# A layer norm's variance moved to tokens on partitions, and the last stage's weight preparation moved into the attention before it

## The reference

```
mu  = mean(x, axis=-1);  var = mean(square(x - mu))
xn  = (x - mu) * rsqrt(var + LN_EPS) * gamma + beta
q, k, v = xn @ Wq + bq, xn @ Wk + bk, xn @ Wv + bv      # 8 heads
x = x + softmax(q k^T / sqrt(dk)) v                     # summed over groups, reshaped
```

```
z = sigmoid(x_t @ W_z + h @ U_z + vz);  r = sigmoid(x_t @ W_r + h @ U_r + vr)
h = (1 - z) * h + z * tanh(x_t @ W + (r * h) @ U + vh)
gate = h @ Wg + routing_bias                            # top 4 of 8 experts, swiglu
```

## Time and profile before

| | us |
|---|---|
| median of 3 runs | 2818.0 (2813.54 to 2818.51) |
| the profiled execution | 2814.62 |
| its span, first to last instruction | 2812.6 |
| layer norm block | from 1415.8 to 1468.4 |
| attention block | to 1636.3 |
| weights block | to 1657.1 |
| rows block | to 1668.4 |

### The profile page before, as it was taken

The page is one execution under the profiler, slowest core; times in us unless marked ns, Lnnn a source line. Parts: engine busy times, 40 slices in busy tenths (PEclk is TensorE's granted clock), DMA queues, the critical chain, the costliest instruction groups (busy, mean ns, idle before and its releaser), DMA issues. The chain is left out here.

```text
span 2812.6 us, 119114 instructions
## 1 busy us (share of the span) xinstructions
PE 2424.7 (86%) x50764; PEld 2022.1 (72%) x50764; DVE 1965.6 (70%) x7376; ACT 1144.6 (41%) x3659; POOL 431.1 (15%) x404
## 2 busy tenths in 40 slices
PE   1678999999999999987547846999999999999999
PEld 0455677777777777654216636999999999999998
DVE  4567777777777777787578736777766777777775
ACT  3124555555555555566126623333333333333333
POOL 0000000000000000000029910222222222222222
PEclk9778999999999999999669967999999999999999
DMA  5000000000000000000013332000000000000000
GB/s 166 2 2 2 5 5 5 5 5 5 5 5 5 5 5 5 5 5 4 3 69 87 88 90 57 9 9 9 11 9 9 9 9 9 9 9 9 5 5 6
DMA packets 52745, 53.77 MB, mean 19 GB/s; under 512 B 24678, under 2 KB 46839, under 8 KB 50041
## 3 DMA queue, kind: packets, MB, share of 16 engines
q1 hardware_dynamic: 47284, 27.79, 3.6%
q0 software_dynamic: 2000, 14.68, 1.5%
q10 hardware_dynamic: 2934, 3.69, 0.4%
HBM read 39.59 MB, written 6.55 MB: 16 GB/s over the span
## 5 line engine op out<-in xcount | busy, mean ns | idle before, releaser
L103 PE MATMUL p<-g_hl,m_h 128*128 128x128 f16 x3072 | 528.7, 219 | 0.0
L103 PE MATMUL p<-g_hh,m_h 128*128 128x128 f16 x3072 | 528.7, 219 | 0.0
L103 PE MATMUL p<-g_hh,m_l 128*128 128x128 f16 x3072 | 528.6, 219 | 0.0
L765 DVE STREAM_TRANSPOSE gt<-lg_b 128x512 f32<-128x512 f32 x324 | 230.3, 711 | 216.5 <-PE lg_b L448 202.6
L1928 POOL TENSOR_TENSOR a_l<-a,a_h 128x384 f16<-128x384 f32 x256 | 233.9, 914 | 915.9 <-ACT a_h L1886 915.9
L642 ACT ACTIVATE gl<-gt 128x128 f32<-128x128 f32 x324 | 100.2, 309 | 629.2 <-DVE gt L765 629.1
L657 ACT ACTIVATE hm<-xy,b 128x512 f32<-128x512 f32 x512 | 347.4, 678 | 0.1
L103 PEld LDWEIGHTS p<-g_hh,m_h 128*128 128x128 f16 x3072 | 300.4, 98 | 1.8
L103 PEld LDWEIGHTS p<-g_hh,m_l 128*128 128x128 f16 x3072 | 300.6, 98 | 0.7
L103 PEld LDWEIGHTS p<-g_hl,m_h 128*128 128x128 f16 x3072 | 300.7, 98 | 0.0
L448 PE MATMUL lg_b<-a_wh_hi,lh 128*32 128x256 f16 x4096 | 217.4, 291 | 79.0 <-DVE lh L789 76.8
(11 more groups left out here) (421 smaller groups left out, 6900.7 us busy)
## 6 DMA issues: line engine op xcount, KB each, us to landing
m_stage<-in_m_w POOLq DMA_DIRECT2D x12, 1024.0 KB, 5.3
hs<-in_m_w SPq DMA_DIRECT2D x16, 384.0 KB, 3.2
xs<-in_x POOLq DMA_DIRECT2D x1, 2048.0 KB, 8.4
x_dram<-x SPq DMA_DIRECT2D x16, 128.0 KB, 2.2
s_v<-in_l_wv SPq DMA_DIRECT2D x1, 2048.0 KB
attention_dram<-att SPq DMA_DIRECT2D x16, 128.0 KB, 2.7
attr<-attention_dram SPq DMA_DIRECT2D x128, 16.0 KB, 1.7
x2r<-x_dram SPq DMA_DIRECT2D x16, 128.0 KB, 2.5
```

The costliest lines, as they stand in the source:

```text
L103: ins = pe.matmul(out, w[wp](k), x[xp](k), start=start, stop=last and k == KT - 1 and xp == 1, skip_group_check=True)
L765: dve.transpose(gt[:, :], lg_b[slot // QS % 2][:, :, :, :].rearrange("p g a x -> p (g a x)"))\
```

## The change

**Layer norm.** The mean is made and subtracted as before, for all four tiles first and in place. ScalarE squares. The variance is made with the squares as the stationary matrix and one column of `mean_w` moving, so that each token's variance stands on its own partition: 16 columns for 2048 tokens, 32 products. Root, reciprocal and Newton step work on 128x16. VectorE multiplies the result with the identity matrix, 128 tokens at a time, into diagonal matrices, and PE multiplies these by `mean_w`, which spreads each token's value over all partitions, into the bank that held the mean. The factor 1/256 is taken out by `gscale` = 256 gamma. ScalarE adds beta. The splits of q and k come before the reductions of v.

```diff
+            NB = W // P
+            sq = [prob[:, :, :, :].rearrange("p k s n -> p k (s n)"),
+                  st.enter_context(nc.sbuf_tensor("ln_sq", [P, KT, W], F32))[:, :, :]]
+            diag = [sq[j // 2][:, j % 2, :] for j in range(NJ)]
+            va, y, yy = (st.enter_context(nc.sbuf_tensor("ln_" + n, [P, NJ * NB], F32)) for n in ("va", "y", "yy"))
...
+            gscale = st.enter_context(nc.sbuf_tensor("ln_gscale", [P, KT], F32))
+            mean = [b[:, :, :].rearrange("p s n -> p (s n)") for b in sc]
+            var = pj[:, :, :].rearrange("p s n -> p (s n)")
...
                 for j in range(NJ):
-                    if j + 1 < NJ:
-                        means(j + 1)
                     pe.wait_ge(sq_ready, j + 1)
-                    if j >= 2:
-                        pe.wait_ge(va_ready, j - 1)
-                    for k in range(KT):
-                        last = pe.matmul(var[j % 2], mean_w[:, :], sq[:, k, :], start=(k == 0), stop=(k == KT - 1))
+                    for u in range(NB):
+                        n = j * NB + u
+                        for k in range(KT):
+                            last = pe.matmul(var[:, n:n + 1], sq[j % 2][:, k, u * P:(u + 1) * P], mean_w[:, 0:1],
+                                             start=(n == 0 and k == 0), stop=(k == KT - 1), skip_group_check=True)
                     last.then_inc(var_pe, 1)
+                pe.wait_ge(d_ready, NJ)
+                for j in range(NJ):
+                    pe.wait_ge(turned, j + 1)
+                    pe.matmul(mean[j], mean_w[:, :], diag[j], start=True,
+                              stop=True).then_inc(spread, 1)
...
-                    if j >= 1:
-                        act.wait_ge(var_pe, j)
-                    act.activation(sq, dd[:, j % 2], ACT.Square).then_inc(sq_ready, 1)
-                    act.wait_ge(var_pe, j + 1)
                     if j >= 2:
-                        act.wait_ge(scaled, 2 * (j - 1))
-
-                    act.activation(va[:, j % 2, :], var[j % 2], ACT.Relu, bias=eps[:, :]).then_inc(va_ready, 1)
-                    act.wait_ge(va_ready, j + 1)
-                    act.activation(root[:, j % 2, :], va[:, j % 2, :], ACT.Sqrt).then_inc(root_ready, 1)
+                        act.wait_ge(var_pe, j - 1)
+                    act.activation(sq[j % 2], x(j), ACT.Square).then_inc(sq_ready, 1)
                 act.wait_ge(loaded, 16 * len(loads))
+                for n, (src, hi, _lo) in enumerate(jobs[:2]):
+                    act.activation(hi, src, ACT.Copy, scale=S).then_inc(hi_done, 1)
+                act.wait_ge(var_pe, NJ)
+
+                act.activation(va[:, :], var[:, 0:NJ * NB], ACT.Relu, bias=eps[:, :]).then_inc(va_ready, 1)
+                act.wait_ge(va_ready, 1)
+                act.activation(y[:, :], va[:, :], ACT.Sqrt).then_inc(root_ready, 1)
                 act.wait_ge(v_sum, KT + 1)
                 act.wait_ge(ready, 3)
-                for src, hi, _lo in jobs:
+                for src, hi, _lo in jobs[2:]:
                     act.activation(hi, src, ACT.Copy, scale=S).then_inc(hi_done, 1)
-
-            @block.gpsimd
-            def _(pool):
-                pool.wait_ge(affine, 32)
+                act.wait_ge(affine, 32)
                 for j in range(NJ):
                     for k in range(KT):
-                        pool.wait_ge(scaled, 2 * j + k + 1)
-                        pool.tensor_scalar(x(j)[:, k, :], xg[:, k, :], beta[:, k:k + 1], None, ALU.add).then_inc(kept, 1)
+                        act.wait_ge(scaled, 2 * j + k + 1)
+                        act.activation(x(j)[:, k, :], x(j)[:, k, :], ACT.Identity, bias=beta[:, k:k + 1])
 
             @block.vector
             def _(dve):
-                def centre(j):
-                    if j >= 2:
-                        dve.wait_ge(sq_ready, j - 1)
-                        dve.wait_ge(scaled, 2 * (j - 1))
-                    dve.wait_ge(mean_pe, j + 1)
-                    dve.tensor_tensor(dd[:, j % 2], x(j), mean[j % 2].unsqueeze(1).to_broadcast([P, KT, W]),
-                                      ALU.subtract).then_inc(d_ready, 1)
+                def low(n):
+                    src, hi, lo = jobs[n]
+                    dve.wait_ge(hi_done, n + 1)
+                    dve.scalar_tensor_tensor(out=lo, in0=src, scalar=S, in1=hi, op0=ALU.mult,
+                                             op1=ALU.subtract).then_inc(lo_done, 1)
 
                 dve.memset(mean_w[:, :], 1.0 / D).then_inc(ready, 1)
 
                 dve.memset(eps[:, :], 4 * LN_EPS).then_inc(ready, 1)
                 dve.memset(brow[:, :], 0.0).then_inc(ready, 1)
                 dve.memset(ones2[:, :], 1.0)
+                for j in range(NJ):
+                    dve.wait_ge(mean_pe, j + 1)
+                    dve.tensor_tensor(x(j), x(j), mean[j].unsqueeze(1).to_broadcast([P, KT, W]),
+                                      ALU.subtract).then_inc(d_ready, 1)
                 dve.wait_ge(affine, 32)
-                centre(0)
-                for j in range(NJ):
-                    if j + 1 < NJ:
-                        centre(j + 1)
-                    v, y = va[:, j % 2, :], root[:, j % 2, :]
-                    dve.wait_ge(root_ready, j + 1)
-                    if j >= 1:
-                        dve.wait_ge(scaled, 2 * j)
-                    dve.reciprocal(y, root[:, j % 2, :]).then_inc(steps, 1)
-
-                    dve.wait_ge(steps, NST * j + 1)
-                    dve.tensor_tensor(yy[:, :], y, y, ALU.mult).then_inc(steps, 1)
-                    dve.wait_ge(steps, NST * j + 2)
-                    dve.scalar_tensor_tensor(out=yy[:, :], in0=yy[:, :], scalar=-0.5, in1=v, op0=ALU.mult,
-                                             op1=ALU.mult).then_inc(steps, 1)
-                    dve.wait_ge(steps, NST * j + 3)
-                    dve.scalar_tensor_tensor(out=y, in0=yy[:, :], scalar=1.5, in1=y, op0=ALU.add,
-                                             op1=ALU.mult).then_inc(steps, 1)
-                    dve.wait_ge(steps, NST * j + 4)
-                    if j >= 1:
-                        dve.wait_ge(kept, 2 * j)
-                    for k in range(KT):
-                        dve.scalar_tensor_tensor(out=xg[:, k, :], in0=dd[:, j % 2, k, :], scalar=gamma[:, k:k + 1],
-                                                 in1=y, op0=ALU.mult, op1=ALU.mult).then_inc(scaled, 1)
+
+                dve.tensor_scalar(gscale[:, :], gamma[:, :], float(D), None, ALU.mult).then_inc(steps, 1)
                 dve.wait_ge(loaded, 16 * len(loads))
-
+                dve.tensor_reduce(s_b[0:1, 2 * D:3 * D], s_b8[0:1, :, :], AX_X, ALU.add).then_inc(v_sum, 1)
+                for n in range(2):
+                    low(n)
                 for k in range(KT):
                     dve.tensor_reduce(s_v[:, k, :], s_v8[:, k, :, :], AX_X, ALU.add).then_inc(v_sum, 1)
-                dve.tensor_reduce(s_b[0:1, 2 * D:3 * D], s_b8[0:1, :, :], AX_X, ALU.add).then_inc(v_sum, 1)
-                for n, (src, hi, lo) in enumerate(jobs):
-                    dve.wait_ge(hi_done, n + 1)
-                    dve.scalar_tensor_tensor(out=lo, in0=src, scalar=S, in1=hi, op0=ALU.mult,
-                                             op1=ALU.subtract).then_inc(lo_done, 1)
+                dve.wait_ge(root_ready, 1)
+                dve.reciprocal(y[:, :], y[:, :]).then_inc(steps, 1)
+
+                dve.wait_ge(steps, 2)
+                dve.tensor_tensor(yy[:, :], y[:, :], y[:, :], ALU.mult).then_inc(steps, 1)
+                dve.wait_ge(steps, 3)
+                dve.scalar_tensor_tensor(out=yy[:, :], in0=yy[:, :], scalar=-0.5, in1=va[:, :], op0=ALU.mult,
+                                         op1=ALU.mult).then_inc(steps, 1)
+                dve.wait_ge(steps, 4)
+                dve.scalar_tensor_tensor(out=y[:, :], in0=yy[:, :], scalar=1.5, in1=y[:, :], op0=ALU.add,
+                                         op1=ALU.mult).then_inc(steps, 1)
+                dve.wait_ge(steps, 5)
+                for j in range(NJ):
+                    dve.tensor_tensor(diag[j].rearrange("p (u n) -> p u n", n=P), ident[:, :].unsqueeze(1).to_broadcast([P, NB, P]),
+                                      y[:, j * NB:(j + 1) * NB].unsqueeze(2).to_broadcast([P, NB, P]),
+                                      ALU.mult).then_inc(turned, 1)
+                for n in (2, 3):
+                    low(n)
+                for j in range(NJ):
+                    dve.wait_ge(spread, j + 1)
+                    for k in range(KT):
+                        dve.scalar_tensor_tensor(out=x(j)[:, k, :], in0=x(j)[:, k, :], scalar=gscale[:, k:k + 1],
+                                                 in1=mean[j], op0=ALU.mult, op1=ALU.mult).then_inc(scaled, 1)
```

(82 more changed lines are left out.)

171 lines of the change are left out of this document (56 added, 115 removed).

## The result

The changed kernel takes 2802.4 us (median of 8 runs, 2792.9 to 2808.4), the kernel before 2815.1 beside it. The medians are 12.7 us apart (0.5%); the ratio on record, which is not the quotient of the medians, is 0.9929 with a 95% interval of 0.9904 to 0.9953 (0.7%, 20 us). It is faster, by a third to a half of the forecast gain of 38 us, and its median lies 12 us above the upper end of the forecast range. The profiled execution took 2808.4 us with a span of 2806.6, 6.0 less than before.

What follows compares the result with a forecast made beforehand. VectorE was taken to set the layer norm's time; weights and rows blocks ran beside nothing. Layer norm -18.6, attention +10.3, weights block -20.8, rows block -1.7, first piece -6.9 sum to -37.7 us: forecast 2777, own range 2772 to 2782.

Steps and rivals of the forecast that it cites:

- The layer norm's size: Layer norm block: reciprocal and Newton step once on 128x16 make it 18.6 us shorter (ends -14 and -21).
- The weights block: Block preparing the last stage's weights, beside which nothing runs: it goes, -20.8 us.
- the first piece: Last stage's first step: ScalarE's 6.95 us wait for the first piece of `m_w3` goes, -6.9 us.
- C: Layer norm: variance at half clock throughout, root at 1443, +5 us, 2782; chance 0.09.
- D: Attention: PE at half clock throughout, +60 us, 2837; chance 0.01.
- E: Last stage's first step finds another stall of 7 us, so the boundary gains don't come, 2784; chance 0.05.
- One of the signs that I had named for a wrong forecast: Attention: the forecast is wrong if the clock there is more than 0.05 lower.
- Attention gets the work that was moved: Attention block: loads, low parts, `vps` and PE's warmer start together add 10.3 us (ends +3 and +22).
- Low parts on VectorE: Attention's batch 2: seven low parts, 3.7 us pitch plus 4.9 waiting, less 1.8 slack: +6.8 us (ends +1 and +13).
- rival A: Attention: low parts wait for the rest of GpSimd's instruction, 11 us for five, with a clock dip +9, 2786; chance 0.19.
- `vps`, +3.6: Attention at g = 58: product takes 4.5 us at full clock, some 0.9 absorbed: +3.6 us (ends +2 and +8).
- PE enters warm: Attention's start: PE comes from the spreading matmuls, perhaps warm, where the first 3 us ran at half clock: -0.5 us.

Runs made afterwards that it cites:

- the three pairs of profiles above: Batches 2 to 7 with low parts beside GpSimd against without: 129.8 and 133.2 us against 116.0, and 130.7 against 117.0.
- the hold run: Changed kernel with GpSimd held before its fifth piece until VectorE has written the seven low parts: 2785.3 us, 0.9886.
- `vps` at the end: Changed kernel with the `vps` product issued behind the last `values` product of attention: 2789.9 us, 0.9898.
- in lots: Changed kernel with the 36 `vps` instructions split into six lots of six, behind the projections of g = 57 to 62: 2794.9 us, 0.9927.
- the first wait: GpSimd's first operation held until VectorE has split x for batches 0 and 1: changed kernel 2796.4 us (0.9910); kernel before with new layer norm 2797.5 us (0.9910).
- the run with the block alone: Kernel before with only the new layer norm block, the last stage's weights staying in their own block: 2809.2 us, 0.9970.
- the four profiles with 17.8: Four of nine profiled kernels, the same program up to g = 16, whose second batch took 17.8 us; in the others 21 to 24.
- memsets: GpSimd's three operations on every weight piece replaced by memsets: changed kernel 2779.0 us (0.9852), kernel before 0.9994, kernel before with new layer norm 2800.3 us (0.9917).

## Why the prediction was wrong

**Right.** The layer norm's size (-19.6 for -18.6): of the 64 variance instructions the first 16 took 1.84 us, the next 3.06 and the last two lots 3.55 each, so the clock fell earlier than I had it, by 16 instructions. The root came at 1439.6; the block began 2.2 us later than before, so this is 1437.4 on the forecast's clock, for 1438. The weights block (-20.8), the rows block (-1.3 for -1.7) and the first piece (-7.1 for -6.9) came as worked out; rivals C, D and E are out, E by the 3.06 us between the first two `zr`. One of the signs that I had named for a wrong forecast came: attention's clock fell by 0.13, to 0.77, not by at most 0.05.

**The step that failed is "Attention gets the work that was moved": 10.3 us in the sum, with an upper end of 22, where 39.7 came.** In its terms:
- *Low parts on VectorE, +6.8 with an upper end of 13.* They cost 14 to 17 us, by the three pairs of profiles above. The forecast took 3.7 us of pitch plus 0.98 us of waiting for each of five. Pitch cost nothing (the hold run), and the waits were 16.1 us over all seven (11.1 with `vps` at the end, 11.1 with it in lots, 9.9 with the first wait), the two small ones too, for which none was put down: `s_rl` alone lost 2.9. I had the right mechanism in rival A and chose the median extra of an `xn_l` over it; the eight `xn_l` hold two of 1.07 that met no wait. The pair of instructions in which I saw the two-input rule agree with the trace was an `xn_h`, which has one input, so it spoke for the other kind of wait. A's 11 us for five lies nearer to the 12.2, 8.0, 8.0 and 9.0 that the five took in the same runs, but by luck in part: it takes a 5.4 us instruction of GpSimd's as closed to its end, and it is not (last section). With some 3.5 us of it closed, A's formula gives an estimate of 1.4 us for a wait, 7 for five and 10 for seven.
- *What follows from it.* PE waits longer and its clock goes from 0.84 to 0.63 in the third batch; I put 3 us on a dip. The third batch is no sum of waits: it took 36.7 us with 16.1 of them and 37.3 with 11.1. How the rest divides between ScalarE's waits, PE's clock and the later splits stays open.
- *`vps`, +3.6, at full clock "that the last batch has".* It had it for 2.6 us. The product took 7.0 us in the changed kernel (1635.46 to 1642.46), ScalarE waited 7.36 us for a transpose, and the batch grew by 9.3. This is just past the bound of 8 that I kept for half clock: the clock of a stretch was carried over to work of another kind put into it, and the clock stayed low behind it (0.60 from 1642.46 on).
- *"PE enters warm", -0.5.* Here a cost lay that no term had: the first batch's 2.9 us, and in this profile some 10 to 13 of the 27.0 in batches 2 to 7, what is left of them without the low parts' 14 to 17. The layer norm block was costed to its end, and its gain taken as kept. The first splits met GpSimd's chain in a new phase; in the run with the block alone that took back 16 of 19.6 us (7 in the first batch, 9 in the next six), and one wait on GpSimd returned it. The forecast had GpSimd's start in it ("at most 7.9 us later"), but asked only whether GpSimd would be late, not whom it would meet.

Put together: 27.0 and 9.3 for 6.8 and 3.6, and 2.9 for the first batch, give 2777 + 20.2 + 5.7 + 3.4 = 2806; the profiled execution took 2808.4, the blocks ahead 2.2 of it. These are whole batches as measured, so it proves no cause that the sum closes. Runs of the changed kernel came in two lots, 2793 to 2798 and 2807 to 2808. The one profile is of the upper lot. Its second batch holds an `xn_h` of 5.78 and an `xn_l` of 3.85 us where the four profiles with 17.8 have at most 1.4 and 1.1, and `vps` at the end, the same program up to the last batch, took 13.4 us less over batches 2 to 7. That is about the distance of the lots, so they may part there; this is not shown, as no run of the lower lot was profiled.

The Trainium skill (SBUF — State Buffer, Who interferes with whom) has the rule that I gave 0.19 and should have made the forecast: with two SBUF inputs against a GpSimd instruction that reads, the one that comes second blocks for the whole of the first. The trace agrees for `s_rl` (its 3.03 us end at 1545.36, GpSimd's `m_l` at 1545.35). It does not for GpSimd's scaling in place, of whose 5.38 us the last 1.7 or so block no such instruction (last section); there the measurement holds.

## What to carry to other kernels

Before work is put on VectorE, list what GpSimd does in that stretch: in these runs a VectorE instruction with both inputs in SBUF waited for a GpSimd instruction that read SBUF, however small it was itself (3.03 us for 0.14), and the price was a wait for each instruction, not a share of its length. When a block is shortened, look at which engines' chains start at its end and whom they meet in their new phase; if two engines collide and one has time to spare, one semaphore wait on that one may be all it takes: it gave 12 to 17 us in each of two places here, by the ratios or the medians. And a stretch's granted clock belongs to the work that is in it: the last batch's fell from 1.00 to 0.66 with `vps` put in.

## What the runs showed that was not expected

- Two kinds of wait between VectorE and GpSimd. Low parts and `xn_l` (two inputs in SBUF) ran at 0.95 and 1.07 us beside memsets; `xn_h`, with one, ended 0.35 us behind the memset every time. The Trainium skill (SBUF — State Buffer, Who interferes with whom) says both: two SBUF inputs contend only with a GpSimd instruction that reads, and `tensor_scalar` in a 2-port mode with any. These rows agree; that `xn_h` runs in such a mode is taken from the wait, no row shows it.
- Taking all reads off GpSimd in the kernel before gained nothing (0.9994), in the changed kernel 0.8% (0.9852 for 0.9929). A wait can cost nothing until something is added beside it.
- Where the clock was at 1.00 when the f32 product `vps` (36 instructions of a few columns) began, it was at 0.50 within 3.1 us in every profile, in the last batch or behind it, in one block or in lots. With neither the product nor low parts in it the last batch ran at 1.00.
- The two kinds of wait end differently, and this is in no term or rival of the prediction. With `vps` at the end (VectorE, then GpSimd):

```profile
1535.77 3.23 DVE L1507 SCALAR_TENSOR_TENSOR wg<-s_wg,wg 128x16 f16<-128x16 f32 x1
...
1540.12 0.14 DVE L1507 SCALAR_TENSOR_TENSOR s_rl<-s_row,rrow 1x8 f16<-1x8 f32 x1
...
1535.31 5.38 POOL L1250 TENSOR_SCALAR m_stage<-m_stage 128x2048 f32<-128x2048 f32 x1
```

GpSimd's scaling in place ends at 1540.69. `wg` is through at 1539.00, and `s_rl` begins 0.57 us before that end and waits for nothing. Over all the traces, an `xn_l` that began beside this scaling ended 0.86 us before the scaling did or, begun in its last 1.8 us, took its 1.07; beside the cast and `m_l` it ended 0.86 us behind their end. `xn_h` ended 0.35 us behind the scaling's end. So two-input instructions get in some 1.7 us before the recorded end of the scaling and `xn_h` does not. GpSimd's recorded ends are rough, but these distances repeat within 0.03 us. Why they differ is not shown.
